# Per-tile waits for routed-row scatters, and a new order around them on VectorE and ScalarE

## The chip, the cores and the metric

The kernel runs on one core of a Trainium2 chip. The metric is the device time of one execution in microseconds (us). TensorE (PE) multiplies and transposes, VectorE (DVE) and ScalarE (ACT) work element by element, GpSimd (POOL) here mostly issues indirect DMAs, and SyncE (SP) issues the plain ones. Each engine runs its own list of instructions in order and waits on semaphores for the others. A change of 0.2% is 0.55 us.

## What is computed

An image batch of 4 x 128 x 16 x 16 passes a deformable-attention block, a self-attention block over 1024 tokens of 128 channels (8 heads of 16), and a layer of 16 experts with top-2 routing. The change lies between the last two, so only they are shown, cut to the core:

```python
t = t + attention(layernorm(t))                      # 4 images x 256 tokens x 128
x = layernorm(t).reshape(-1, 128)                    # "nrm": the rows that are routed
gate_logits = x @ gate_weight.T                      # 16 experts
top_vals, top_idx = top_k(gate_logits, 2)
routing_w = softmax(top_vals)
h = silu(einsum('td,efd->tef', x, w1))
h_mean = (sum of h over the tokens that chose expert e) / count_e
y_mean = einsum('ef,edf->ed', h_mean, w2)
t = t + sum_k routing_w[k] * y_mean[top_idx[k]]
```

## The kernel before

The 1024 tokens are 8 tiles of 128, in two halves: half 0 is tiles 0 to 3 (images 0 and 1), half 1 tiles 4 to 7. Self-attention runs in 8 units (image x group of four heads), pipelined by hand: step k of `unit_step` on each engine does the scores of unit k, the softmax of unit k - 1 and the outputs of unit k - 2, for k = 0 to 9 (UNITS is 8). Units 0 to 3 make half 0, units 4 to 7 half 1.

The outputs of a unit go this way: TensorE weighs the values (`weigh_values`), ACT copies the result out of PSUM (`unit_out`), TensorE turns it (`turn_out`, L1556), and DVE divides it by the sum of the softmax (`unit_norm`, L1063 the reciprocal and L1065 the multiply). When a half's four units are there, TensorE turns the half's outputs (`turn_outputs`, L1576), ACT copies them to `o_c` (`outputs_out`, L689), and TensorE makes from them the outputs' part of the gate logits (`output_logits`, L1588) and the projection (`project_out`, L1595).

From there a half goes to the experts. On DVE: `input_deviation` (L1081; for half 1 it waits for half 1's `output_logits`), `rank_logits` and `choose` (top 2 of each token), `residual` (L1072, the block's sum `x2_k`), `moments` (L807, L810). TensorE's `rank` (L1608 to L1612) counts, for each token, those before it that chose the same expert. DVE's `place` (L1111 to L1123) turns that into slot numbers, and `experts_of` (L1127 to L1133) notes which expert owns which slots. For the layer norm of the routed rows, ACT takes the root (`root`, L739), DVE the reciprocal and the shift (`scale`, L1139 and L1140), and ACT writes the four normalised tiles (`normalise`, L732), one increment of the semaphore `lnf["norm"]` for each tile.

POOL then scatters the rows: for each tile t and each of the two choices an indirect DMA (L509) writes 128 rows from `nrm` to their slots in DRAM (`scratch`), 16 scatters in all, tiles in order. When the eight scatters of a half have landed, SP reads that half's slots back in three groups of 512 rows (L418). TensorE turns them (`turn_slots`, L1680), ACT copies them (`columns_out`, L776), and each tile of 128 slots is multiplied with its experts' weights (`expert_tiles`, L1697 and L1705). Each tile holds four grains of 32 slots, each with an expert of its own; the weights of three of the four are first copied to fixed places ("staged"), six of these copies by ACT (`stage_first`, L759) and the rest by DVE (`stage`, L1199). ACT applies SiLU (L786); DVE's staging copies and TensorE's later tiles wait for earlier ones. The means, the second expert matrix, the sum over the routing weights and the stores end the kernel.

The order of the work around the change is written out by hand. On DVE it is: step 8 of `unit_step` (with `unit_norm(6)`, then half 0's `rank_logits`, `choose`, `residual`, `moments`), step 9 (only `unit_norm(7)`), `scale(0)`, `place(0)`, `experts_of(0)`, then half 1's `input_deviation` (L1081) and so on to `place(1, lambda: scale(1))`, which has the scale step inside it (`between`, after its second operation). On ACT: `root(0)`, `outputs_out(1)`, `normalise(0)`, two staging copies, `root(1)`, `normalise(1)`, the copies of x2, four staging copies, an exponential and a load of the SiLU table, then `columns_out(0)`. On TensorE: step 9 with `turn_out(7)`, `rank(0)` and `input_logits(1)`, then `turn_outputs(1)`, `output_logits(1)`, `project_out(1)`, `rank(1)`, `turn_x2`, and `turn_slots(0)`. POOL waits ahead of each half for its slot numbers (`slots_ready`) and for all four normalised tiles of the half.

## Time and profile before

| | us |
|---|---|
| median of 3 runs | 275.45 |
| the runs | 275.06 to 275.71 |
| the profiled execution, its own time | 275.87 |
| its span (first to last instruction) | 273.9 |

| engine | busy us | share of the span |
|---|---|---|
| PE, matmuls | 222.5 | 81% |
| PE, weight loads | 154.9 | 57% |
| DVE | 207.4 | 76% |
| ACT | 174.7 | 64% |
| POOL | 48.1 | 18% |

The time of the profiled execution is its span and some 2 us around it. The shares are averages over unlike stages. The stage of this change lies between 200 and 240 us, where no engine is full: there the waits between engines count, and the timelines of each engine show them. Times in the rows are us from the start of the span. TensorE's clock is given as a share of 2.4 GHz: 1.00 is 2.4 GHz and 0.50 is 1.2 GHz.

### The profile page before, as it was taken

How to read it: one execution, taken by the hardware profiler on the slowest of the kernel's cores; microseconds unless marked ns; L12 is line 12 of the kernel's file. 1: busy time of each engine (PE TensorE's matmuls, PEld its weight loads, DVE VectorE, ACT ScalarE, POOL GpSimd, SP SyncE). 2: the span in 40 equal slices, each digit the busy share in tenths (PEclk: the TensorE clock that was granted, in tenths of full speed). 3: DMA queues.
4: the chain of work that ended last, by engine and by line, in shares of the span. 5: the costliest groups of instructions: out<-in, count | busy, mean ns of one | idle time of the engine just before them, and what ended most of it. 6: DMA issues, size and time to landing. Idle time of an engine off the chain costs nothing.

```text
span 273.9 us, 7291 instructions
## 1 busy us (share of the span) xinstructions
PE 222.5 (81%) x2936; PEld 154.9 (57%) x2936; DVE 207.4 (76%) x482; ACT 174.7 (64%) x257; POOL 48.1 (18%) x64
## 2 busy tenths in 40 slices
PE   0799449999999998869999887889987307899985
PEld 0579327666767667637979755566556203233354
DVE  5766888999999999865335967888849957598412
ACT  5366898999999996066442567675667391565610
POOL 7004918910000000010001100000000677100000
PEclk9999859999999999997999999999999855999999
DMA  6930000000000000790000000000000115594002
GB/s 148 357 140 2 0 0 4 2 5 2 2 5 2 2 2 5 243 370 2 0 0 4 0 0 2 0 2 0 2 1 4 38 50 162 153 425 175 0 2 77
DMA packets 8590, 16.38 MB, mean 60 GB/s; under 512 B 752, under 2 KB 5104, under 8 KB 8304
## 3 DMA queue, kind: packets, MB, share of 16 engines
q1 hardware_dynamic: 8048, 14.90, 15.5%
q0 software_dynamic: 512, 1.05, 1.2%
q8 instruction: 23, 0.38, 0.6%
q14 instruction: 7, 0.06, 0.1%
HBM read 12.80 MB, written 3.15 MB: 58 GB/s over the span
## 4 chain that ended last, share of the span: by engine, by line
issue 54%; PE 30%; DVE 8%; ACT 3%; DMA 3%; SPq 1%; DVEq 1%; ACTq 0%
PE ps L1697 8%; PE ps L1380 6%; DVE wide L991 5%; PE ps L1720 2%; DVE msda L996 2%; DMA r_sb<-in_rows 2%; ACT arena L594 1%; PE ps L1760 1%; PE ps L1282 1%; PE ps L1680 1%; PE ps L1366 1%; PE ps L1335 1%; DMA late<-slot_rows 1%; PE ps L1311 1%; PE ps L1323 1%
## 5 line engine op out<-in xcount | busy, mean ns | idle before, releaser
L594 ACT ACTIVATE arena<-ps,one_less_sq 128x1024 bf16<-128x1024 f32 x64 | 67.2, 1112 | 4.7 <-PE ps L1366 4.7
L1380 PEld LDWEIGHTS ps<-arena 128*128 128x128 bf16 x1536 | 43.3, 96 | 19.8 <-issue 10.4
L1380 PE MATMUL ps<-arena 128*128 128x48 bf16 x1536 | 49.4, 184 | 5.1 <-DVE wide L991 4.6
L996 DVE TENSOR_REDUCE msda<-wide 128x768 f32 x32 | 46.1, 1513 | 0.0
L1366 PE MATMUL ps<-wide,sel 64*128 64x512 bf16 x128 | 25.7, 400 | 7.3 <-ACT arena L594 7.3
L991 DVE TENSOR_TENSOR wide<-ps,wide 128x768 f32<-128x768 f32 x32 | 30.1, 1009 | 1.1 <-PE ps L1380 1.1
L509 POOL DMA_INDIRECT slot_rows<-nrm,slots x16 | 16.1, 1006 | 66.2 <-ACT nrm L732 61.7
L1697 PE MATMUL ps<-arena,w_sb 128*32 x48 | 23.5, 636 | 1.0 <-ACT sel L786 1.0
L1046 DVE TENSOR_REDUCE t_k<-ps 128x2 f32<-128x512 f32 x32 | 20.5, 684 | 0.0
L668 ACT ACTIVATE wide<-ps 128x512 f32<-128x512 f32 x32 | 17.3, 594 | 1.4 <-PE ps L1526 1.3
L1705 PE MATMUL ps<-late,w_sb 128*32 128x512 f32 x80 | 16.6, 667 | 0.0
L1199 DVE COPY late<-arena 128x512 f32 x34 | 12.0, 423 | 4.8 <-PE ps L1705 3.0
L1021 DVE SCALAR_TENSOR_TENSOR wide<-ps,v_sb,wide 128x512 f32<-128x512 f32 x8 | 5.9, 750 | 11.8 <-ACT wide L640 9.2
L1039 DVE SCALAR_TENSOR_TENSOR xm<-ps,raw_by,xm 128x512 fp32r<-128x512 f32 x16 | 11.9, 748 | 3.7 <-ACT xm L657 1.9
L1697 PEld LDWEIGHTS ps<-arena,w_sb 128*32 128x32 f32 x48 | 5.4, 117 | 16.3 <-issue 16.3
L786 ACT ACTIVATE sel<-ps 128x512 f32<-128x512 f32 x12 | 6.9, 601 | 9.7 <-PE ps L1705 9.7
L1680 PE MATMUL ps<-ident,late 128*128 128x128 f32 x24 | 4.5, 330 | 10.1 <-DMA late<-slot_rows 10.1
L1366 PEld LDWEIGHTS ps<-wide,sel 64*128 64x128 bf16 x128 | 6.2, 93 | 11.1 <-ACT arena L594 7.7
L660 ACT ACTIVATE xm<-ps,high_by 128x512 fp32r<-128x512 f32 x8 | 5.5, 686 | 10.5 <-PE ps L1488 10.5
L495 POOL MEMSET t_k<- 128x1024 f32 x1 | 1.0, 952 | 63.4 <-PE ps L1426 63.4
L640 ACT ACTIVATE wide<-ps,v_sb 128x512 f32<-128x512 f32 x8 | 5.4, 694 | 9.6 <-PE ps L1444 9.6
L1680 PEld LDWEIGHTS ps<-ident,late 128*128 128x128 f32 x24 | 3.2, 166 | 13.0 <-issue 13.0
(320 smaller groups left out, 510.7 us busy)
## 6 DMA issues: line engine op xcount, KB each, us to landing
arena<-in_w_t SPq DMA_DIRECT2D x1, 4096.0 KB, 13.6
wide<-in_w_t SPq DMA_DIRECT2D x1, 4096.0 KB, 15.2
w_sb<-in_weights SPq DMA_DIRECT2D x1, 1544.0 KB, 8.8
slot_rows<-t_c SPq DMA_DIRECT2D x2, 768.0 KB, 10.4
late<-slot_rows SPq DMA_DIRECT2D x6, 256.0 KB, 3.3
x_sb<-in_x SPq DMA_DIRECT2D x4, 128.0 KB, 2.3
out<-xn SPq DMA_DIRECT2D x4, 128.0 KB, 1.8
r_sb<-in_rows SPq DMA_DIRECT2D x1, 288.0 KB, 4.7
```

Of the source, the lines that this page charges most:

```text
L509: nc.gpsimd.indirect_dma_start(out=scratch[h], out_offset=bass.IndirectOffsetOnAxis(ap=slots[:, c, t:t + 1], axis=0), in_=nrm[:, t, :], in ...
L594: nc.scalar.activation(hot[:, u, c:c + 5:4, :, :], ps[:, 2 * (c % 2):2 * (c % 2) + 2, :].rearrange("r p (b q) -> r p b q", b=B), ACT.Relu, ...
L668: nc.scalar.activation(prob_t[u % 2][:, i, :], ps[:, 2 + i % 2, :], ACT.Exp).then_inc(prob_ready, 1)
L991: nc.vector.tensor_tensor(prod[:, c, :, :, :], g, w.unsqueeze(3).to_broadcast([P, 2, NP * NK, DH]), ALU.mult).then_inc(g_free, 1)
L996: nc.vector.tensor_reduce(msda[:, 4 * c + u:4 * c + u + 3:2, bass.ds(i, 1), :].rearrange("q b h d -> q b (h d)"), prod[:, c, :, :, :].rear ...
L1039: nc.vector.scalar_tensor_tensor(out=to, in0=ps[:, 6 + of_keys, :].rearrange("c (n t) -> c n t", n=2), scalar=raw_by[:, of_keys:of_keys + ...
L1046: nc.vector.tensor_reduce(nmax[:, :, 2 * (u % 2) + i // 2, HROWS * (i % 2) + SPLIT], ps[:, i % 2, :].rearrange("q (t k) -> q t k", t=2), A ...
L1199: nc.vector.tensor_copy(staged_at[n % len(staged_at)], w1_sb[:, bass.ds(at[q][t % GROUP], 1), :].rearrange("d e f -> d (e f)")).then_inc(s ...
L1366: ins = nc.tensor.matmul(ps[:, 2 * (c % 2) + a, :], sel[rows, i % 4, c, :], terms_t[rows, i // 4, u * HALF:(u + 1) * HALF])
L1380: ins = nc.tensor.matmul(ps[:, 4 + b, p * NK * DH:(p + 1) * NK * DH], hot[:, u, p, b, :], rhs, start=(s == 0), stop=(s == PARTS - 1))
L1697: nc.tensor.matmul(ps[0:GRAIN, 2 + t % 4, :], x_cols[:, t * P:t * P + GRAIN], w1_sb[:, bass.ds(at[j], 1), :].rearrange("d e f -> d (e f)"))
L1705: ins = nc.tensor.matmul(ps[GRAIN * q:GRAIN * (q + 1), 2 + t % 4, :], x_cols[:, t * P + GRAIN * q:t * P + GRAIN * (q + 1)], staged_at[entr ...
```

## The change

- POOL waits for the normalised rows of one tile ahead of that tile's two scatters, and for the slot numbers once in a half, as before.
- On ACT `normalise(0)` comes ahead of `outputs_out(1)`.
- On DVE step 9 of `unit_step` does nothing any more; `place(0)` comes directly after step 8, with `scale(0)` inside it as half 1 has it, and `unit_norm(7)` follows it, ahead of `experts_of(0)`.

```diff
@@ POOL
                 h = t // 4
                 if t % 4 == 0:
                     pool.wait_ge(slots_ready, h + 1)
-                    pool.wait_ge(lnf["norm"], 4 * (h + 1))
+                pool.wait_ge(lnf["norm"], t + 1)
@@ ACT
             root(0)
+            normalise(0)
             outputs_out(1)
-            normalise(0)
@@ DVE, unit_step
-                if k >= 2:
+                if 2 <= k <= UNITS:
                     unit_norm(k - 2)
@@ DVE
-            scale(0)
-            place(0)
+            place(0, lambda: scale(0))
+            unit_norm(UNITS - 1)
             experts_of(0)
```

## Rows read from the trace of the kernel before

**Rows 1.** Chain that ended last, in order of time: start us, us, what.

```profile
224.85 2.78 DMA late<-slot_rows
...
236.02 0.61 ACT sel L786
```

**Rows 2.** Timeline of POOL, 180 to 232: start us, us, instruction [idle before <-releaser].

```profile
213.32 1.22 POOL L509 DMA_INDIRECT slot_rows<-nrm,slots  x1 [61.66 <-ACT nrm L732]
...
222.41 1.08 POOL L509 DMA_INDIRECT slot_rows<-nrm,slots  x1 [0.31 <-issue]
223.79 0.96 POOL L509 DMA_INDIRECT slot_rows<-nrm,slots  x1 [0.30 <-issue]
```

**Rows 3.** Timeline of ACT, 180 to 246.

```profile
209.14 0.30 ACT L739 ACTIVATE lnf_std<-lnf_mv,eps_c 128x4 f32<-128x4 f32 x1 [0.89 <-DVE lnf_mv L810]
210.30 0.60 ACT L689 ACTIVATE xn<-ps 128x512 f32<-128x512 f32 x1 [0.87 <-PE ps L1576]
210.80 1.64 ACT L732 ACTIVATE nrm<-t_k,lnf_shift,lnf_rstd 128x128 f32<-128x128 f32 x4
...
218.32 1.65 ACT L732 ACTIVATE nrm<-t_k,lnf_shift,lnf_rstd 128x128 f32<-128x128 f32 x4 [0.63 <-issue]
...
228.97 0.60 ACT L776 ACTIVATE w_sb<-ps 128x512 f32<-128x512 f32 x1 [2.93 <-PE ps L1680]
```

**Rows 4.** Instructions of the tile nrm, 205 to 235: ns min/median/max, first and last start.

```profile
L732 ACT ACTIVATE nrm<-t_k,lnf_shift,lnf_rstd x8: 478/482/493, 210.8 to 219.5; 128x128 f32<-128x128 f32 x8
```

**Rows 5.** Timeline of DVE, 180 to 246.

```profile
209.02 0.17 DVE L1063 RECIPROCAL inv_sum<-ps 128x8 f32<-128x8 f32 x1
...
209.76 0.17 DVE L1111 TENSOR_SCALAR quads_e<-ps 128x16 f32<-128x16 f32 x1
...
210.42 0.42 DVE L1117 TENSOR_REDUCE first_slot<-quads_before 128x16 f32<-128x256 f32 x1
...
211.46 0.29 DVE L1123 TENSOR_REDUCE slots<-picked_slot 128x8 int32<-128x128 f32 x1
...
213.01 0.22 DVE L1081 TENSOR_TENSOR lg<-ps,ln_std 128x64 f32<-128x64 f32 x1
...
217.91 0.18 DVE L1139 RECIPROCAL lnf_rstd<-lnf_std 128x4 f32<-128x4 f32 x1
218.12 0.16 DVE L1140 SCALAR_TENSOR_TENSOR lnf_shift<-lnf_mv,lnf_rstd 128x4 f32<-128x4 f32 x1
218.20 0.41 DVE L1117 TENSOR_REDUCE first_slot<-quads_before 128x16 f32<-128x256 f32 x1
...
219.23 0.29 DVE L1123 TENSOR_REDUCE slots<-picked_slot 128x8 int32<-128x128 f32 x1
...
232.40 0.76 DVE L1199 COPY msda<-arena 128x512 f32 x2
```

**Rows 6.** Timeline of PE, 180 to 246.

```profile
208.63 0.25 PE L1612 MATMUL ps<-pair_sq,ones_b 128*128 128x64 bf16 x4
...
209.63 0.64 PE L1576 MATMUL ps<-ident,msda 128*128 128x128 f32 x4
210.95 1.06 PE L1588 MATMUL ps<-gate_o,xn 128*128 128x16 f32 x8 [0.69 <-ACT xn L689]
211.87 1.14 PE L1595 MATMUL ps<-w_sb,xn 128*128 128x128 f32 x8
215.50 0.18 PE L1608 MATMUL ps<-ceil_b,ones_b 128*128 128x16 bf16 x1 [2.49 <-DVE pair_sq L1104]
...
227.84 1.94 PE L1680 MATMUL ps<-ident,late 128*128 128x128 f32 x8 [10.09 <-DMA late<-slot_rows]
...
236.86 0.61 PE L1697 MATMUL ps<-arena,w_sb 128*32 x1 [1.05 <-ACT sel L786]
```

**Rows 7.** Stretches: busy us of PE, PEld, DVE, ACT, POOL, granted clock, DMA share, GB/s.

```profile
212.00:218.00 6.00, 2.98 (x23) 2.29 (x22) 5.55 (x33) 1.88 (x5) 3.77 (x4) 0.87 0.11 33
...
232.00:234.00 2.00, 2.00 (x16) 0.52 (x12) 1.16 (x4) 0.00 (x0) 1.68 (x2) 0.62 0.11 33
```

## The prediction

> **What bounds the kernel now.** I read the chain of work that ended last first. From the reload of the routed rows on it is one piece: a 256 KB read-back (2.78 us) issued at 224.85, TensorE's transposes of those rows at 227.84, expert tiles 0 to 3, the first SiLU at 236.02, expert tile 4 at 236.86, and from there TensorE nearly without a hole [rows 1, 6]. TensorE stood idle for 10.09 us ahead of 227.84 and was released by that read-back [rows 6], so everything after it moves with the read-back. The read-back waits for the eight scatters of half 0, so the timeline of POOL comes next: the first scatter starts at 213.32, the eighth ends at 222.41 + 1.08 = 223.49, and the ninth (half 1) follows with a gap of 0.30 [rows 2]. POOL's own work is a closed queue of one scatter per (223.79 - 213.32) / 8 = 1.31 us, and the read-back lands 4.14 us after the eighth ends (224.85 + 2.78 = 227.63). What sets the end is therefore when the first scatter starts.
>
> Its releaser is read in the timelines of ACT and DVE. The four normalisations of half 0 start at 210.80 and end at 212.44 [rows 3], each 0.48 long [rows 4]; the slot numbers of half 0 start at 211.46 and are there at 211.75 [rows 5]. POOL starts 213.32 - 212.44 = 0.88 after the last of them. The row of tile 0 was ready at 210.80 + 0.48 = 211.28.
>
> **The change part by part, in the profiled execution.**
>
> *Wait of one tile.* The first scatter needs the slot numbers (211.75) and tile 0's row (211.28), no longer the fourth row (212.44). Alone: 212.44 - 211.75 = 0.69 earlier. The rows follow at under 0.41 us each, the scatters at two per tile, so no later tile waits. Six more waits are executed, three in half 0. The trace doesn't show POOL executing a met wait apart from its instruction; the gap of 0.30 between scatters is the nearest row, so three of them cost 0 to 0.9 us at the most; I take 0, since the ninth scatter, at which the kernel before passes both of its waits, has the same 0.30 ahead of it as the eighth [rows 2]. The start-up of 0.88 stays; a wake-up by DVE may differ from one by ACT, for which I allow one such gap, 0.3, either way.
>
> *DVE.* The last unit's reciprocal and multiply leave the place ahead of half 0's slot numbers. They and the scale step take 209.76 - 209.02 = 0.74, the scale step 0.29 of it, so the two are 0.45. The chain of place took from 209.76 to 211.75, that is 1.99; with the scale step inside it takes 1.99 + 0.29 (217.91 to 218.20, where half 1 already runs so) = 2.28 [rows 5]. It now begins at 209.02, so the slot numbers are there at 211.30, 0.45 earlier. The scale step comes 0.66 into the chain (209.76 to 210.42), at 209.68; the root that it needs ended at 209.44 [rows 3], so it doesn't wait, and rank(0) ended at 208.63 + 0.25 = 208.88 [rows 6]. The shift is ready after 0.21 and 0.16 more (217.91, 218.12), at 210.05.
>
> *ACT.* Normalisation follows the shift by 0.04 (218.12 + 0.16 = 218.28, then 218.32, in half 1 [rows 3, 5]) and starts at 210.09 instead of 210.80; tile 0's row is there at 210.57, the fourth at 211.73. All rows now precede the slot numbers or their own scatter. This part gives nothing by itself; it is needed, because the outputs' copy now waits for a late transpose and would hold the rows to 213.1.
>
> Sum on the path: first scatter 0.88 after 211.30, at 212.18: **1.14 us earlier** than 213.32. The read-back and TensorE's restart follow at 226.70.
>
> *What is paid: half 1.* The unit's multiply ended at 209.52, 0.50 after its reciprocal began; that now begins 0.20 after the last operation of place starts (211.01), so the multiply ends at 211.71. TensorE's transposes of half 1's outputs start at 211.83 instead of 209.63, the copy on ACT at 212.50 instead of 210.30, the outputs' logits at 213.15 instead of 210.95, each step with its old distance [rows 3, 6]. DVE is done with experts_of(0) at 213.01 as before (the same instructions in another order) and then waits for these logits (about 1.06 long, so 214.27): the next step slips from 213.01 by D = 1.26 [rows 5, 6]. Queued behind it on DVE are half 1's choice, residual, moments, slot numbers, the gap, and the staging copies; on TensorE rank(1) and turn_x2; on ACT root, normalise(1), x2_out, four staging copies and two table loads. All slip by D.
>
> Who waits for that? (a) POOL's ninth scatter, wanted at 222.65: half 1's slot numbers end at 219.52 + D = 220.8, and tile 4's row earlier still, so 1.9 us are left. (b) ACT must be free for the copy of the first transposed rows. It started that copy at 228.97 after 2.93 of idle [rows 3], free since 226.04: slack 2.93 before, 2.93 - 1.14 = 1.79 with TensorE 1.14 earlier. (c) DVE's staging copies for tile 4, done by 232.40 + 0.76 = 233.16, against 236.86 [rows 5, 6]: slack 3.7, later 2.6. So the gain on the path is min(1.14, 2.93 - D), and with D = 1.26 all of 1.14 arrives.
>
> *The clock.* The new idle stretches of TensorE run from about 209.7 (the transposes that began at 209.63 now come later) to 211.83 and 212.5 to 213.15, with the later one (213.01 to 215.50 before [rows 6]) shrinking to about 1.4. In the trace the granted clock averages 0.87 over 212 to 218, so it fell from 2.4 to 1.2 GHz at about 216.4, after that long idle stretch; it rose at about 233.5 (mean 0.62 over 232 to 234), with TensorE at work from 227.84 [rows 6, 7]. With a long idle stretch now 213.01 - 209.7 = 3.3 us earlier, the fall may come that much earlier, around 213, on the outputs' logits of half 1. At 1.2 GHz eight passes of this kind take 1.94 (the transposes at 227.84) instead of 1.06 [rows 6], so D goes up to 1.26 + 0.9 = 2.2, and the gain is 2.93 - 2.2 = 0.75. The fall can land anywhere between, so I take the middle of 1.14 and 0.75: **0.95 us**. The Trainium skill (TensorE: Matmul & The Clock Gate, HAM oscillation) says that idle between bursts sends the array back to the low clock; it speaks against this change, which puts a hole in work that was dense, and the rows of the fall at 216.4 agree.
>
> *A second rule against it.* The scatters that ran beside DVE's staging copies took 0.96 to 1.08 (those at 223.79 and 222.41 [rows 2]); the first, beside small operations, took 1.22. The copies are now D later and the scatters 1.14 sooner, so fewer scatters of half 0 stand beside a copy; I take nothing, bound +0.12, the 1.08 over the 0.96. The Trainium skill (DMA: Bandwidth & Descriptors, SWDGE vs HWDGE vs iDMA) says that DVE in its two-port mode locks GpSimd out of the SBUF in which it writes its descriptors; by that the scatters beside the copies would grow, and the rows show no more than the 0.12.
>
> **The rivals.**
> 1. *The clock takes or gives the difference.* TensorE restarts 1.14 earlier, but its first four tiles run at 1.2 GHz until the rise. If the rise stays at 233.5, the time from 226.70 to 233.5 is 6.8 at half rate instead of 5.7: only 0.57 arrives, 274.9. If it comes 2 us sooner than the restart's shift explains, another 1.0 is saved: 2.1 in all, 273.3. For: the trace shows one such rise, and nothing ties it to the restart. Together 0.25, about equal parts.
> 2. *Slower: the half-1 work on ACT becomes the bound.* Place: the copy of the first transposed rows behind ACT's table loads, which end at 226.04 + D. It decides from D = 2.93. If the low clock holds over the outputs' logits, their projection, rank and the transposes of x2, and each of these is waited for in turn, D is 1.26 + 0.9 + 1.0 + 0.8 = 4.0 and the kernel is 1.1 slower, 276.5. Against: projection (old start 211.87) runs beside DVE's choice, which hides it. 0.11.
> 3. *The edit doesn't move the first scatter.* If POOL's 0.88 isn't a wake-up but work that ended independently of ACT, or if the extra waits cost the 0.9, then 0 to 0.3 is left: 275.3. For: nothing in the trace tells what the 0.88 is. 0.10.
> 4. *The first SiLU isn't released by TensorE's start.* Tile 0's products come first of four tiles after 227.84, yet the SiLU that reads them starts at 236.02 [rows 1], when TensorE is through with all four. If what holds them is not bound to the restart, nothing arrives: 275.4. For: I can't explain the hold; against: it ends just as TensorE's burst ends, which moves. 0.06.
>
> **How the numbers follow.** The profiled execution took 275.87 (span 273.9 and 1.97 around it), 0.42 above the median 275.45; the shift is taken off the median: 275.45 - 0.95 = 274.5. Chance of this case 0.48, with its own range 274.0 to 274.9. Range for 8 in 10: down to the early rise (273.3, less 0.1 for a D of 1.26) and up to the rival without effect, 275.7. A change of 0.2% is 0.55 us, about what a measurement can tell from none: faster means under 274.9, slower over 276.0. Faster: 0.48 less 0.05 at its edge, 0.13 and 0.06 of rival 1, 0.62 in all; slower: rival 2 and scatter of runs, 0.12; the rest 0.26.
>
> **What would show it.** First scatter near 212.2, started by DVE's slot numbers and not by ACT; eight scatters of 1.31; read-back near 223.7; transposes near 226.7; the first SiLU about 1 us earlier. DVE idle about 1.2 (full clock) to 2.2 us ahead of L1081, released by TensorE's L1588. ACT's copy of the first transposed rows with under 2 us idle before it; none left means D reached 1.79. The prediction is wrong if the first scatter stays at 213.3, if that copy waits for ACT, or if the clock's rise moves by more than the restart.

## The result and the profile after

The changed kernel takes 279.87 us (median of 5 runs, 279.44 to 281.49) against 275.45 for the kernel before: the ratio is 1.0161, with a 95% interval of 1.0113 to 1.0208. It is 4.4 us slower, where 0.95 us faster was predicted. The profiled execution of after took 279.87 with a span of 277.8, 3.9 us more than the span of before. The ratios and intervals here and below leave out executions over 1.5% above the fastest of their kernel; the lists of runs show all.

The page of after, its span and busy times:

```profile
span 277.8 us, 7292 instructions
...
PE 228.5 (82%) x2936; PEld 158.4 (57%) x2936; DVE 207.4 (75%) x482; ACT 175.3 (63%) x257; POOL 47.9 (17%) x64
```

VectorE and ScalarE do the same work as before. TensorE shows 6 us more for the same 2936 instructions: more of them ran at the low clock. That is no cause yet: it can follow from new waits just as well.

I read after in the order of the prediction's sum. The timeline of POOL (start us, us, instruction, [idle before <-releaser]), first and ninth scatter:

```profile
212.26 1.22 POOL L509 DMA_INDIRECT slot_rows<-nrm,slots  x1 [60.45 <-ACT nrm L732]
...
222.72 0.96 POOL L509 DMA_INDIRECT slot_rows<-nrm,slots  x1 [0.30 <-issue]
```

The first scatter starts 1.06 earlier than in [rows 2]; 1.14 was predicted (212.18). The queue is as closed as before: (222.72 - 212.26) / 8 = 1.31. So what the change is about arrived. TensorE's timeline, from half 1's outputs to the next tiles:

```profile
211.90 0.66 PE L1576 MATMUL ps<-ident,msda 128*128 128x128 f32 x4 [1.98 <-DVE msda L1065]
213.25 1.80 PE L1588 MATMUL ps<-gate_o,xn 128*128 128x16 f32 x8 [0.69 <-ACT xn L689]
...
226.59 2.17 PE L1680 MATMUL ps<-ident,late 128*128 128x128 f32 x8 [6.14 <-issue]
231.54 1.05 PE L1697 MATMUL ps<-arena,w_sb 128*32 x1 [2.77 <-issue]
...
237.92 0.66 PE L1680 MATMUL ps<-ident,late 128*128 128x128 f32 x4
...
239.65 1.05 PE L1705 MATMUL ps<-t_k,w_sb 128*32 128x512 f32 x3
...
244.32 0.66 PE L1680 MATMUL ps<-ident,late 128*128 128x128 f32 x4
```

Half 1's transposes start at 211.90 (211.83 predicted). The restart is at 226.59 (226.70 predicted, 227.84 in [rows 6]), 1.25 ahead of before. But then the expert tiles, which followed the transposes directly in before, start at 231.54: 2.77 us of idle have come between them. Tile 4 begins at 239.65 where before had it at 236.86, and the next group's transposes stand at 244.32 against 240.43. From there to the end the distance stays 3.9. **All of the loss arises between 228.8 and 244.3**, and the reason is in what ACT and DVE did there. The places in before that I compare with, on TensorE and DVE:

```profile
229.72 1.06 PE L1697 MATMUL ps<-arena,w_sb 128*32 x1
```

```profile
225.88 0.16 DVE L1180 TENSOR_SCALAR expert_of<-expert_of 128x12 f32<-128x12 f32 x1
...
231.72 0.76 DVE L1199 COPY t_k<-arena 128x512 f32 x2 [1.46 <-issue]
```

ACT in after:

```profile
228.23 0.20 ACT L772 ACTIVATE table_junk<-eps_c 128x1 f32<-128x1 f32 x1
230.80 0.60 ACT L776 ACTIVATE w_sb<-ps 128x512 f32<-128x512 f32 x1 [2.37 <-remote]
235.10 0.60 ACT L776 ACTIVATE w_sb<-ps 128x512 f32<-128x512 f32 x1 [3.71 <-remote]
235.59 1.08 ACT L786 ACTIVATE sel<-ps 128x512 f32<-128x512 f32 x2
```

ACT is free at 228.43. The transposes that its two copies wait for ended by 226.59 + 2.17 = 228.76, the first four of them about half way. Yet the copies start at 230.80 and 235.10. In before the first of them started as soon as four transposes were through (228.97, [rows 3]). DVE:

```profile
228.27 0.16 DVE L1180 TENSOR_SCALAR expert_of<-expert_of 128x12 f32<-128x12 f32 x1
229.38 0.56 DVE L1181 TENSOR_TENSOR t_k<-expert_of,expert_f 128x384 f32<-128x384 f32 x1 [0.95 <-DVE expert_of L1180]
...
232.20 0.17 DVE L1129 TENSOR_TENSOR end_slot<-end_slot,first_slot 128x16 f32<-128x16 f32 x1 [2.07 <-remote]
233.61 0.36 DVE L1130 TENSOR_TENSOR ended<-end_slot,slot_no 128x192 f32<-128x192 f32 x1 [1.24 <-DVE end_slot L1129]
235.01 0.35 DVE L1132 TENSOR_REDUCE expert_of<-ended 128x12 f32<-128x192 f32 x1 [1.04 <-DVE ended L1130]
...
239.17 0.76 DVE L1199 COPY t_k<-arena 128x512 f32 x2 [1.47 <-issue]
```

This is `experts_of(1)` and the counts after it, a chain in which each instruction waits for an increment of DVE's own semaphore by the one before. At L1181 the releaser is DVE's own L1180, which was done at 228.43, and the wait lasts until 229.38. Four such waits add up to 0.95 + 2.07 + 1.24 + 1.04 = 5.3 us. In before the same instructions follow each other without a wait. So an instruction waits for an increment whose producer is through, 1 to 2 us on DVE (from itself) and longer on ACT (from TensorE): the first copy starts some 3 us after its four transposes were through, the second 6.3 us after the last transpose. I call this **the hold** below. POOL is in the second half of its scatters then. The view of waits, 226 to 241 (engine, line <- releaser: us in total, times, longest), shows the same from the other side:

```profile
ACT w_sb L776 <- remote: 6.1, 2, 3.7
...
DVE end_slot L1129 <- remote: 2.1, 1, 2.1
...
PEld ps L1705 <- DVE t_k L1199: 1.2, 2, 1.0
```

"Remote" means that no instruction of this core's engines ended just ahead of the release. No other core runs here, so I read the word as the mark of a late arrival, not of a sender.

### The profile page after: what moved, and what is told of

It reads as the page before. It is cut to its first block, busy times and chain, and to the rows that moved or that the text cites. A ratio compares the mean times of both kernels' runs of the same rounds, so it can differ in the third digit from the quotient of the medians.

```text
span 277.8 us, 7292 instructions
## 1 busy us (share of the span) xinstructions
PE 228.5 (82%) x2936; PEld 158.4 (57%) x2936; DVE 207.4 (75%) x482; ACT 175.3 (63%) x257; POOL 47.9 (17%) x64
## 4 chain that ended last, share of the span: by engine, by line
PE 48%; DVE 20%; issue 17%; ACT 9%; DMA 2%; DVEq 1%; SPq 1%; ACTq 1%; another core or an unknown queue 1%
PE ps L1380 5%; PE ps L1697 5%; DVE wide L991 4%; DVE t_k L1046 3%; PE ps L1488 3%; PE ps L1454 3%; PE ps L1541 2%; PE ps L1720 2%; DVE msda L996 2%; PE ps L1502 2%; PE ps L1266 2%; PE ps L1705 2%; PE ps L1514 2%; PE ps L1444 2%; DMA r_sb<-in_rows 2%
## 5 line engine op out<-in xcount | busy, mean ns | idle before, releaser
L996 DVE TENSOR_REDUCE msda<-wide 128x768 f32 x32 | 45.1, 1452 | 0.0
L991 DVE TENSOR_TENSOR wide<-ps,wide 128x768 f32<-128x768 f32 x32 | 29.1, 948 | 1.2 <-PE ps L1380 1.2
L1697 PE MATMUL ps<-arena,w_sb 128*32 x48 | 24.9, 659 | 2.8 <-issue 2.8
L1705 PE MATMUL ps<-late,w_sb 128*32 128x512 f32 x80 | 18.0, 688 | 0.0
L1488 PE MATMUL ps<-z_h,wqk_h 128*128 128x256 f32 x32 | 10.4, 325 | 0.0
```

Source lines behind the costliest of these rows:

```text
L991: nc.vector.tensor_tensor(prod[:, c, :, :, :], g, w.unsqueeze(3).to_broadcast([P, 2, NP * NK, DH]), ALU.mult).then_inc(g_free, 1)
L996: nc.vector.tensor_reduce(msda[:, 4 * c + u:4 * c + u + 3:2, bass.ds(i, 1), :].rearrange("q b h d -> q b (h d)"), prod[:, c, :, :, :].rear ...
L1488: ins = nc.tensor.matmul(ps[:, 6 + of_keys, j * HW:(j + 1) * HW], w[:, at_w:at_w + P], z[:, b * HW:(b + 1) * HW], start=(n == 0), stop=(n ...
L1697: nc.tensor.matmul(ps[0:GRAIN, 2 + t % 4, :], x_cols[:, t * P:t * P + GRAIN], w1_sb[:, bass.ds(at[j], 1), :].rearrange("d e f -> d (e f)"))
L1705: ins = nc.tensor.matmul(ps[GRAIN * q:GRAIN * (q + 1), 2 + t % 4, :], x_cols[:, t * P + GRAIN * q:t * P + GRAIN * (q + 1)], staged_at[entr ...
```

## The experiments

Executions of one kernel vary here by up to 7 us; those of the kernel before lie between 274.95 and 279.56, 19 of all 79 at 278.6 and above. That upper group reaches the times of after, and none of its executions was profiled, so whether it is the same loss isn't known. The work ahead of the first scatter varies by over 1 us from one profile to the next with nothing changed in it. So traces are compared from a common point, the first scatter: its start, and the tail from there to the end of the span. The "first SiLU" column is its distance from the first scatter. Ratios are against the kernel before, run beside each on the same chip. Each row of the trace columns is one execution, and not always a typical one.

| kernel | first scatter | first SiLU | tail | span | ratio of the times [95%] |
|---|---|---|---|---|---|
| before | 213.32 | +22.70 | 60.6 | 273.9 | 1 |
| after | 212.26 | +23.33 | 65.5 | 277.8 | 1.0161 [1.0113, 1.0208] |
| e1_waits_alone | 212.35 | +22.82 | 60.6 | 273.0 | 0.9988 [0.9935, 1.0042] |
| e2_orders_alone | 213.91 | +22.98 | 60.9 | 274.8 | 1.0125 [1.0031, 1.022] |
| e3_pe_kept_busy | 213.64 | +23.21 | 64.8 | 278.4 | 1.0136 [1.0045, 1.0226] |
| e4_half1_scatters_late | 213.79 | +19.11 | 66.6 | 280.4 | 1.0241 [1.0141, 1.0342] |
| e5_few_increments_after | 211.22 | +23.20 | 66.1 | 277.3 | 1.0118 [1.0032, 1.0204] |
| e6_few_increments_before | 214.56 | +22.85 | 60.7 | 275.3 | 1.0019 [0.9964, 1.0074] |
| e7_waits_few_increments | 212.99 | +22.75 | 62.3 | 275.3 | 0.9979 [0.9934, 1.0024] |
| e8_half1_late_by_filler | 211.80 | +22.80 | 65.1 | 276.9 | 1.0109 [1.006, 1.0158] |
| e9_clock_kept_before | 215.00 | +26.87 | 67.6 | 282.6 | 1.0223 [1.0135, 1.031] |
| e10_twelve_scatters | 213.73 | +19.91 | 62.4 | 276.1 | 0.9992 [0.9944, 1.0041] |
| e11_chain_ahead_after | 212.54 | +23.35 | 64.2 | 276.7 | 1.0217 [1.0125, 1.0309] |
| e12_chain_ahead_waits | 214.34 | +23.02 | 60.9 | 275.2 | 1.001 [0.998, 1.004] |
| e13_twelve_scatters_before | 214.66 | +18.15 | 58.2 | 272.9 | 0.9949 [0.9924, 0.9974] |
| e14_clock_kept_shorter | 214.59 | +24.25 | 66.1 | 280.7 | 1.0165 [1.0045, 1.0285] |
| e15_dve_chain_late | 214.52 | +22.95 | 62.5 | 277.0 | 0.9997 [0.9946, 1.0047] |

**The parts alone: e1 and e2.** e1 is the kernel before with the new waits on POOL alone, e2 the changed kernel with the old waits, that is the new orders on DVE and ACT alone.

```diff
                     pool.wait_ge(slots_ready, h + 1)
-                    pool.wait_ge(lnf["norm"], 4 * (h + 1))
+                pool.wait_ge(lnf["norm"], t + 1)
```

> The kernel before with the wait for one tile's rows as its only change. The trace of the changed kernel shows its first scatter 1.06 us earlier, as forecast, and yet 4 us lost, most of it behind increments of semaphores by TensorE and VectorE that other engines see 1 to 2 us late between 228 and 235 us. Theory A (held increments are set off by where the scatters of half 1 stand against TensorE's turning of the slots and VectorE's chain of small operations): the scatters are only 0.7 us earlier and VectorE's chain isn't late, so the result is open between -0.7 us (no longer hold than before) and +2 (hold moves onto VectorE's chain as well). Theory B (the loss comes from half 1's work being 2.15 us late): -0.7 us, 274.8. First scatter at 212.6.

> The changed kernel with the old wait for all four rows: only the new orders on VectorE and ScalarE. The first scatter starts at 212.7 (0.88 after the fourth row at 211.86). Theory B (half 1's lateness makes the loss): within 0.5 us of the changed kernel, 279.4 to 280.3, with L1081 at 215.2. Theory A (the place of the scatters against the chains decides): anything between 275 and 280, with a hold that shows as idle time of VectorE in its linked operations or of ScalarE ahead of L776.

In e1's trace the first scatter starts 0.97 earlier than in before and the span is 0.9 shorter, with the tail the same. ACT's first SiLU in e1:

```profile
235.17 2.07 ACT L786 ACTIVATE sel<-ps 128x512 f32<-128x512 f32 x4 [5.42 <-PE ps L1705]
```

It has the idle time of [rows 1] again ahead of it and has moved by 0.85. So the path argument holds for the waits, though ten runs (274.49 to 278.31) don't separate the gain of the times from nothing. e2 took 276.88 to 281.46 and is slower by its times, but its profiled execution was its fastest run, with a tail of only 60.9: DVE's chain lost 0.5 in it and ACT nothing. Half 1 was as late in it as in after (L1081 2.96 after the first scatter, 2.90 in after) and the staging copies for tile 4 started 22.27 after the first scatter, 3.87 later than in before, at no cost. So in this execution the lateness stayed within the slack that the prediction reckoned. The loss comes with the new orders, then, and not in every execution. How much of the 1.0161 the waits add to e2's 1.0125 these intervals don't tell.

**The clock: e3.** The changed kernel with dummy multiplications on TensorE in its idle stretches, so that it keeps 2.4 GHz over half 1's logits.

```diff
+            keep_clock(9, 2)
             turn_outputs(1)
+            keep_clock(3, 2)
             output_logits(1)
             project_out(1)
+            keep_clock(5, 2)
             rank(1)
```

> The changed kernel with dummy bf16 multiplications of TensorE into an unused PSUM bank in its new idle stretches: 9 ahead of the turn of half 1's outputs, 3 ahead of the outputs' logits, 5 ahead of rank(1). The granted clock should stay at 2.4 GHz over half 1's logits, so L1081 slips by 1.26 instead of 2.15 us. Theory B: half 1's lateness makes the loss, so 1 us or more comes back, under 279.0. Theory A: what is held isn't bound to this lateness, so the gain is anything from 0 to 4 by where the hold falls; if the hold stays and shows the same idle times (2.4 and 3.7 us ahead of L776), under 0.9 us comes back.

The clock stayed at 2.4 GHz until about 222, and L1081 came 215.80 - 213.64 = 2.16 after the first scatter instead of 2.90 in after. The tail is 64.8, the ratio 1.0136. ACT's copies (L776) still stood for 2.72 and 3.00 and DVE's chain for some 4.4. The fall of the clock ahead of half 1's logits is not what costs the 4.4 us, unless the dummies cost what the clock gives back, which this run can't exclude.

**The scatters: e4.** The changed kernel with POOL's ninth scatter held back until ACT has made both of its copies.

```diff
                     pool.wait_ge(slots_ready, h + 1)
+                if t == 4:
+                    pool.wait_ge(cols_ready, 2)
```

> The changed kernel, but the eight scatters of half 1 start only when ScalarE has copied the first two groups of slots. No scatter runs beside TensorE's first turning of slots and VectorE's second experts_of. Theory A (scatters in flight hold the increments of TensorE and VectorE): the idle of ScalarE ahead of its two copies L776 falls from 2.4 and 3.7 us to under 1.5 and 0.5, and VectorE's linked operations L1181, L1129, L1130, L1132 lose their waits of 1 to 2 us. Theory C (the hold is independent of the scatters, of the read-back or of a queue of semaphores): the waits stay. The whole time is longer in both, because the read-back of half 1 comes late; only the holds are looked at.

ACT's copies and the first SiLU, then a step of DVE's chain, then the ninth scatter (lines are 2 higher than in after):

```profile
230.19 1.06 ACT L778 ACTIVATE w_sb<-ps 128x512 f32<-128x512 f32 x2
...
232.90 0.60 ACT L788 ACTIVATE sel<-ps 128x512 f32<-128x512 f32 x1 [1.65 <-PE ps L1707]
```

```profile
231.10 0.18 DVE L1131 TENSOR_TENSOR end_slot<-end_slot,first_slot 128x16 f32<-128x16 f32 x1
```

```profile
232.37 0.95 POOL L511 DMA_INDIRECT slot_rows<-nrm,slots  x1 [8.52 <-issue]
```

With no scatter running, both of ACT's copies go back to back, DVE's chain has no wait, and the first SiLU stands 19.11 after the first scatter instead of 22.70, in the kernel before, or 23.33. As soon as the scatters resume, waits of this kind come back: the fourth SiLU, at 240.90, has 3.99 of idle ahead of it. Half 1 is late now, so the kernel as a whole is slower (282.47 and 282.92). **The hold goes with the scatters.**

**The number of increments: e5, e6, e7.** TensorE's transposes of slots and of x2 increment a semaphore eight and four at a time; here only the last of each four does. e5 is the changed kernel so, e6 the kernel before, e7 the kernel before with the new waits.

```diff
-            nc.tensor.transpose(slots_bank(g)..., x_slots[...], ident[:, :]).then_inc(cols_mm, 1)
+            ins = nc.tensor.transpose(slots_bank(g)..., x_slots[...], ident[:, :])
+        ins.then_inc(cols_mm, 1)
...
-        act.wait_ge(cols_mm, GROUP * g + GROUP)
+        act.wait_ge(cols_mm, g + 1)
```

> The changed kernel with one increment for each group of four transposes (turn_slots and turn_x2) instead of four. Without half 1's scatters in flight the holds were gone, so the scatters cause them. Theory A1 (TensorE's increments queue up behind the scatters and are let out one at a time, some 1.4 us apart, and VectorE's linked operations wait in the same queue): with a quarter of the increments the copy of the first group starts within 0.6 us of ScalarE being free, the second within 1.5 us of its transposes, VectorE's chain loses less than 2 us instead of 5, and the kernel takes 275 to 277.5. Theory A2 (the hold belongs to the stretch of the scatters alone, however many increments there are): the idle times and 279 to 281 stay.

> The kernel before with one increment for each four transposes. The runs of the kernel before lie in two groups, 275.0 to 276.2 and 278.6 to 279.4. A1: the upper group becomes rare and the median of the lower one stays within 0.4 us of 275.4. A2: both groups stay with about a third of the runs in the upper.

> The kernel before with the wait for one tile's rows and with one increment for each four transposes. A1: 274.4 to 275.2, below both kernels, with few runs over 276. A2: as the wait alone, whose ten runs lie between 274.5 and 278.3 with a median of 276.65.

Nothing of substance moved. e5 is as slow as after (279.25 to 281.28), with 2.64 and 2.97 ahead of ACT's copies and 1.21, 1.72 and 2.08 in DVE's chain. e6 equals the kernel before, and in e7, too, the first SiLU keeps its +22.75. The Trainium skill (VectorE: DVE Perf Modes, the section on the TRN2 errata) warns that a high rate of increments by one engine can deadlock another, and that dense increments by several engines should be spaced. Nothing deadlocked here; if the hold were a mild form of that, e5 and e6 should have lost it, and they didn't. e7's profile shows one thing more, in the view of stretches (busy us of PE, PEld, DVE, ACT, POOL, clock, DMA share, GB/s):

```profile
238.00:240.00 2.00, 2.00 (x16) 0.54 (x12) 1.93 (x6) 1.38 (x3) 0.00 (x0) 0.50 1.23 391
```

TensorE, idle for 2.17 ahead of tile 4, fell back to 1.2 GHz for about 3.4 us, where it stood at 1.00 in the kernel before. At half rate that is some 1.7 us (an estimate from these rows), as much as e7's tail of 62.3 is over 60.6.

**Lateness alone: e8.** The kernel before with DVE's order and POOL's waits untouched, the new order on ACT, and dummy multiplications ahead of half 1's transposes, so that half 1 comes late with TensorE's clock up.

```diff
             root(0)
-            outputs_out(1)
             normalise(0)
+            outputs_out(1)
...
+            keep_clock(10, 2)
             turn_outputs(1)
```

> The kernel before with ScalarE's new order, and with ten dummy multiplications of TensorE ahead of the turn of half 1's outputs; VectorE's order and the wait for four rows stay. Half 1's logits come about 2.1 us late as in the changed kernel, with TensorE at 2.4 GHz, and the first scatter starts at about 212.7. Theory L (the loss is made by half 1's lateness, which puts TensorE's increments and VectorE's second chain into the stretch in which the scatters hold them): 278 to 281, as the new orders alone (276.9 to 281.5). Rival (it is the new order on VectorE or the low clock that loses): within 1 us of the kernel before, under 276.5.

The logits ran at the high clock, and DVE's chain was held:

```profile
212.28 1.06 PE L1588 MATMUL ps<-gate_o,xn 128*128 128x16 f32 x8 [0.69 <-ACT xn L689]
```

```profile
231.75 0.56 DVE L1181 TENSOR_TENSOR t_k<-expert_of,expert_f 128x384 f32<-128x384 f32 x1 [1.85 <-remote]
...
234.54 0.17 DVE L1234 TENSOR_TENSOR cnt<-cnt,cnt_half 128x16 f32<-128x16 f32 x1 [1.98 <-remote]
...
237.17 0.76 DVE L1199 COPY t_k<-arena 128x512 f32 x2 [1.46 <-issue]
```

```profile
237.65 1.59 PE L1706 MATMUL ps<-t_k,w_sb 128*32 128x512 f32 x3 [1.16 <-DVE t_k L1199]
```

The tail is 65.1, the ten runs lie between 278.57 and 281.7, and the ratio is 1.0109 [1.006, 1.0158]. Neither the new waits nor DVE's new order is in this kernel, and its dummies end at 211.2, ahead of the first scatter. **Half 1 being late is enough** for two thirds of the loss by the times, though not in every execution (e2's profile). The path is DVE's chain: it lost 4.9 in four held waits, the staging copies for tile 4 came 25.37 after the first scatter, and TensorE waited for them until +25.85, 2.3 later than in before. ACT's own copies were held for under 1 us, and the first SiLU kept its +22.80. The tail is 4.5 longer than that of before, but up to 1.7 of this is another fall of the clock (0.50 over 238 to 240), which after doesn't have.

**The clock raised for the tiles: e9 and e14.** The kernel before with ten dummy multiplications between `project_out(1)` and `rank(1)`, and more of them (40 in e9, 14 in e14) ahead of `turn_slots(0)`, to raise the clock for tiles 0 to 3.

```diff
             project_out(1)
+            keep_clock(10, 2)
             rank(1)
...
+            keep_clock(40, 2)
             turn_slots(0)
```

> The kernel before with dummy multiplications of TensorE ahead of rank(1) (10) and ahead of the first turning of slots (40), so that it restarts at 2.4 GHz or gets there sooner. Theory H: the first SiLU is released by the end of the hold, 22.7 us after the first scatter, and not by TensorE's speed, so nothing is gained: 275.0 to 276.5, with a longer wait of ScalarE ahead of the first SiLU. Rival C (the low clock over the first four tiles is on the path): 1.4 to 2.8 us faster, 272.6 to 274.1.

TensorE turned to the slots only at 237.97, so e9 says nothing on the clock. But it shows the hold in a new place. Of the 40 dummies 35 were through by 228.62, 0.22 each, and at that pace the last five would have ended at 229.7, about when the read-back was there. Instead each of the five stood, and DVE's chain with them:

```profile
233.68 0.59 PE L1388 MATMUL ps<-ones_b,ident_b 128*128 128x512 bf16 x1 [1.75 <-issue]
235.85 0.58 PE L1388 MATMUL ps<-ones_b,ident_b 128*128 128x512 bf16 x1 [1.58 <-issue]
237.27 0.58 PE L1388 MATMUL ps<-ones_b,ident_b 128*128 128x512 bf16 x1 [0.83 <-issue]
```

```profile
235.14 0.18 DVE L1234 TENSOR_TENSOR cnt<-cnt,cnt_half 128x16 f32<-128x16 f32 x1 [2.75 <-remote]
235.87 0.17 DVE L1235 TENSOR_SCALAR cnt<-cnt 128x16 f32<-128x16 f32 x1 [0.55 <-DVE cnt L1234]
237.26 0.25 DVE L1236 RECIPROCAL inv_cnt<-cnt 128x16 f32<-128x16 f32 x1 [1.22 <-DVE cnt L1235]
```

The kernel gives these dummies no semaphore to wait for and none to increment. So the hold isn't only on increments that come late: it also stops instructions of TensorE that wait for nothing in the kernel, and both engines go on at the same instants (235.85 and 235.87, 237.27 and 237.26). And since TensorE sends no increment in this stretch, its increments aren't the cause of DVE's waits.

> The kernel before with dummy multiplications of TensorE ahead of rank(1) (10) and ahead of the first turning of slots (14 instead of 40). TensorE restarts with the read-back as in the kernel before. Theory H: its clock doesn't matter, the first SiLU comes at 22.7 after the first scatter and the span ends at 60.6 to 60.9. Rival C (the clock over the first four tiles is on the path): 1 us or more sooner. If turn_x2 is late through the first ten, x2_out on ScalarE still has 2 us of slack.

e14 took 282.77, 282.18, 284.18 and 278.44. Its profiled execution is one of the long ones:

```profile
232.58 0.17 DVE L1235 TENSOR_SCALAR cnt<-cnt 128x16 f32<-128x16 f32 x1 [0.53 <-issue]
233.29 0.25 DVE L1236 RECIPROCAL inv_cnt<-cnt 128x16 f32<-128x16 f32 x1 [0.53 <-DVE cnt L1235]
234.01 0.20 DVE L1237 TENSOR_SCALAR in_quad<-quad_i 128x64 f32<-128x64 int32 x1 [0.47 <-issue]
```

```profile
236.10 0.60 ACT L776 ACTIVATE w_sb<-ps 128x512 f32<-128x512 f32 x1 [8.79 <-remote]
```

ACT stood idle for 8.79 ahead of this copy. Some 2.8 of it is the ordinary wait for the four transposes, which began at 228.98; the other 6.0 are hold, about as long as the longest one otherwise (6.19 in e11). DVE's chain was held for 1.65 + 0.53 + 0.53 + 0.47 + 1.19 = 4.4, although DVE and ACT have the order of before. I had expected at worst no change. The dummies ended at 221.47, well ahead of the hold, and the fourth run took 278.44, so one trace doesn't show that they cause it. The clock stood at 0.50 over 228 to 242 all the same, so neither e9 nor e14 tests rival C, a faster clock over the first tiles; that stays untested.

**Fewer scatters: e10 and e13.** Tiles 6 and 7 aren't scattered, so 12 scatters run instead of 16; e10 is the changed kernel so, e13 the kernel before.

```diff
-                for c in range(TOPK):
+                for c in range(TOPK if t < 6 else 0):
...
-            sp.wait_ge(scattered[h], 16 * 4 * TOPK)
+            sp.wait_ge(scattered[h], 16 * (4, 2)[h] * TOPK)
```

> The changed kernel without the four scatters of tiles 6 and 7, so their rows are missing in the sums of the experts. In all traces so far held increments of TensorE come through 22.7 us after the first scatter starts, about 2.2 us after the sixteenth ends. Theory H (the hold lasts as long as the stream of scatters and begins in its last quarter): with twelve scatters the stream ends 15.4 us after its start, nothing is held at 16 to 22.7 us; ScalarE copies the first group of slots as soon as it is free, VectorE's linked operations have no waits over 0.3 us, the first SiLU comes within 3 us of TensorE's first expert tile, and the kernel takes under 276, up to 4 us less than the changed kernel. Rival (the scatters are not the cause, it is the read-back or the queue of increments itself): the waits stay and so do 279 to 281.

> The kernel before without the four scatters of tiles 6 and 7 (their rows are missing in the experts' sums). I read each run from its first scatter on, because what lies ahead of it varies by 1.4 us from run to run: in the kernel before and three variants the span ends 60.6 to 60.9 us after the first scatter starts, with the first SiLU at 22.7. Theory H: the hold goes, the first SiLU starts right after tile 0's products, at 18.5 to 19.5, and tile 4 starts as soon as TensorE is through with tile 3 and the next transposes, so the span ends 1 to 2 us sooner, 58.6 to 59.6 after the first scatter. Rival (the hold is hidden in the kernel before): 60.6 to 60.9.

e10, ACT's copies of the first two groups:

```profile
230.91 1.08 ACT L776 ACTIVATE w_sb<-ps 128x512 f32<-128x512 f32 x2
```

They don't wait, and no wait above 0.56 is left in DVE's chain; the first SiLU stands at +19.91. Against the kernel before with its 16 scatters the ratio is 0.9992 [0.9944, 1.0041], where it was 1.0161; the median, 276.87, still misses the "under 276" that I expected. And in e13, the kernel before without the four scatters:

```profile
230.36 0.60 ACT L776 ACTIVATE w_sb<-ps 128x512 f32<-128x512 f32 x1 [2.97 <-PE ps L1680]
...
232.81 0.60 ACT L786 ACTIVATE sel<-ps 128x512 f32<-128x512 f32 x1 [1.00 <-PE ps L1705]
```

The first SiLU comes when TensorE has made its first product, at +18.15 and no longer at +22.70. So the kernel before is held as well: this is what 4.6 of the 5.6 us ahead of its first SiLU were. By the tails the hold costs it 60.6 - 58.2 = 2.4 us, by the times 0.5% [0.3, 0.8], 1.4 us.

e13 is also the kernel that e10 has to be compared with, and there the loss isn't all gone: e10's runs have a median of 276.87 (275.61 to 278.55), e13's of 274.82 (273.37 to 275.34). That is 2.1 us by the medians, 1.2 by the two ratios, and 4.2 by the tails of two single executions (62.4 and 58.2; e10's is one of its long ones). Of the 4.4 us some 2.3 to 3.2 go with the four scatters; 1.2 to 2.1 stay. The traces show where. In e10 ACT gets to its copies only at 230.91, straight from its table loads, 17.18 after the first scatter instead of e13's 15.70, and DVE's staging copies for tile 4 are later still:

```profile
237.47 0.76 DVE L1199 COPY t_k<-arena 128x512 f32 x2 [1.47 <-issue]
```

That is +23.74, against +18.30 in e13, and TensorE takes tile 4 up at +24.25 instead of +21.17. I read this so: with 16 scatters the held first SiLU hides a part of half 1's lateness, and once it comes at +18 to +20, the lateness is more than the slack. A little hold is left in e10 too and adds to it: ACT's second copy of x2 starts 0.57 late at 225.19, given as "remote", and DVE's first staging copies come at +13.31, where they stand at +11.83 in after.

**The chain moved ahead: e11 and e12.** `experts_of(1)` and the counts stand ahead of the staging copies for tiles 1 to 3 instead of behind them, in the changed kernel (e11) and in the kernel before with the new waits (e12).

```diff
+            slot_experts(0)
+            experts_of(1)
+            slot_experts(1)
...
             dve.wait_ge(ld_w1, 16)
             dve.wait_ge(x2_mm, TILES)
...
-            slot_experts(0)
-            experts_of(1)
-            slot_experts(1)
```

> The changed kernel with VectorE's second chain (slot_experts, experts_of(1), the counts, 4.2 us of it) moved ahead of its first staging copies, so it runs 10 to 14 us after the first scatter instead of 16 to 25 us. Theory H: VectorE's chain loses nothing any more (5.3 us of waits in the changed kernel), its copies for tile 4 are ready by the time TensorE wants them, and what is left of the loss is ScalarE's copy of the slots behind TensorE's held increments: 276.5 to 279. Rival (VectorE's chain was covered by the hold of TensorE anyway): 279 to 281 as before the move.

> The kernel before with the wait for one tile's rows and the same move of VectorE's second chain. If the upper group of runs (278.6 to 279.4 in the kernel before, 276.4 to 278.3 with the wait alone) comes from VectorE's chain reaching into the hold, it goes: 274.3 to 275.3, below both kernels. If it comes from TensorE's increments or from the clock, both groups stay as with the wait alone, median 276.65.

A miss: I had looked for the hold from some 15 us behind the first scatter on. In e11 the chain runs from +10 on and is held from +13 to +19, for 1.35, 0.47, 0.46, 1.18 and 1.20; ACT's second copy is held for 6.19, up to 235.39; the staging copies come at 238.05. Its runs lie between 278.74 and 283.96. In e12 the new order neither costs nor brings anything that can be told apart (1.001 [0.998, 1.004]).

**DVE's chain late alone: e15.** The kernel before with six copies without use (2.2 us) ahead of the chain, so that it stands where the changed kernel has it, while ACT and TensorE are as before.

```diff
+            for n in range(6):
+                spare = (y_rest, hat_x, pair)[n % 3]
+                ins = nc.vector.tensor_copy(spare[:, :, :], y_pos[:, :, :])
+                if n % 3 == 2:
+                    link(ins)
             slot_experts(0)
             experts_of(1)
```

> The kernel before with six extra copies (2.2 us) on VectorE ahead of slot_experts(0) alone: VectorE's second chain runs as late as in the changed kernel (15 to 19 us after the first scatter), while TensorE's half 1, ScalarE and the scatters keep their times. Theory V (the loss of the changed kernel is VectorE's chain of linked operations standing in the hold): waits of 1 to 2 us show inside the chain, the copies for tile 4 are late, and the span ends 63 to 66 us after the first scatter; runs 278 to 281. Theory T (TensorE's own late work brings it): the chain is 2.2 us late, hidden by the slack of 3.7 us, and the span ends at 60.6 to 60.9; runs as before.

```profile
233.87 0.25 DVE L1241 RECIPROCAL inv_cnt<-cnt 128x16 f32<-128x16 f32 x1 [0.92 <-DVE cnt L1240]
```

The chain reaches into the hold only with its end and loses 0.92 + 0.93. The staging copies for tile 4 start 22.45 after the first scatter, 4.05 later than in before, and that is hidden behind ACT's held SiLU (ratio 0.9997 [0.9946, 1.0047]). The profile has a tail of 62.5. Up to 1.7 of it (the same estimate) is a fall to 1.2 GHz as in e7:

```profile
239.00:242.00 3.00, 3.00 (x16) 0.81 (x13) 3.00 (x10) 2.00 (x5) 0.00 (x0) 0.50 1.23 309
```

So DVE late by 2.2 is not enough when the hold takes only 1.85 from it. In e8 DVE's chain started as late (L1180 at +14.78, +14.77 here, +12.56 in before) but lost 4.9, and that was enough with ACT's copies hardly held. With 16 scatters what decides seems to be whether the copies for tile 4 come before or after the moment TensorE wants them, some 23.5 after the first scatter: +22.27 in e2 and +22.45 here, +25.37 in e8.

## Why the prediction was wrong

**What was right.** The part of the wait and of DVE's order: first scatter 212.26 for 212.18, eight scatters of 1.31, TensorE's restart 226.59 for 226.70. Half 0's slot numbers were there at 211.12 + 0.29 = 211.41 for 211.30, the whole chain of that execution being some 0.15 later. What was left open on the clock came out at its dear end, and correctly priced:

```profile
212.00:214.00 2.00, 1.31 (x8) 1.08 (x9) 1.31 (x5) 0.60 (x1) 1.44 (x2) 0.84 0.00 0
214.00:218.00 4.00, 3.06 (x16) 2.77 (x17) 2.64 (x18) 1.15 (x2) 3.09 (x4) 0.50 0.21 66
```

The granted clock fell at about 213.4, about 3 us earlier than in before, and the logits took 1.80 instead of 1.06. The delay of half 1 on DVE was this:

```profile
215.16 0.23 DVE L1081 TENSOR_TENSOR lg<-ps,ln_std 128x64 f32<-128x64 f32 x1 [1.71 <-PE ps L1588]
```

D = 215.16 - 213.01 = 2.15, with 2.2 forecast for the low clock. The price of slack (b), ACT's table loads, held too: ACT was free at 228.43, for 226.04 + 2.2 = 228.24 by the sum, and 0.54 ahead of where its first copy stood in before. Without a hold about that much of the gain could have passed ACT, where 0.75 was forecast for the low clock.

**The step that failed** is the sentence that everything after TensorE's restart moves with it, and with it the term min(1.14, 2.93 - D) for the gain. It rests on each increment reaching its waiter at once. From 228.4 on that wasn't so, and I had the sign in front of me: the kernel before had 5.60 us ahead of its first SiLU [rows 1] for a product that TensorE had made by 230.57 + 1.06 = 231.63, 4.4 us earlier. I gave that rival, 4, a chance of 0.06, and let its price be "nothing arrives". The place was right and the price wrong. e4, e10 and e13 show that the wait is bound to the scatters. In before, e1, e2, e6, e7, e8, e12 and e15 it ends 22.7 to 23.0 us after the first of them, 1.5 to 2.4 us after the sixteenth. TensorE's restart keeps its distance from the first scatter in these traces too (14.4 to 14.6), so they alone don't tell the two apart; e13 does, where the restart stands at +14.57 and the SiLU comes at +18.15. So the end of the wait moves with the scatters, and an earlier first scatter should arrive by it, as 0.85 of it did in e1's trace.

**Slack (c)** failed with it, and this is the term that turned a lost gain into a loss. DVE's staging copies for tile 4 were given 3.7 us of slack against a start of 236.86. The slack was read in a trace in which the chain ahead of these copies ends at 230.26, 16.9 after the first scatter, about where DVE's instructions begin to be held in after (its wait at L1181 runs from +16.2 to +17.1). In after half 1's work on DVE is 2.15 late, 2.4 by L1180 (228.27 for 225.88), and the scatters are 1.06 early. The chain starts 16.0 after the first scatter instead of 12.6 and runs into the hold:

| from the first staging copy for tile 4 | us |
|---|---|
| before, 231.72 | |
| half 1 late, D as it stands at L1180 | +2.4 |
| four held increments, 5.3, less the small gaps and durations that stood there before | +5.1 |
| after, 239.17 | +7.45 |

The slack of 3.7 is used up twice. On TensorE's side the sum runs to the same point: its tiles started 231.54 - 229.72 = 1.82 later (ACT's copy held for 2.37), and took 0.87 longer to the end of tile 3 and the four transposes behind it (231.54 to 238.51 against 229.72 to 235.82), since the clock rose only at about 237.3, later in the burst. So TensorE was ready for tile 4 at 238.51 and waited for DVE's copy until 239.65. From there DVE is the bound:

```profile
240.52 2.77 DVE L1199 COPY late<-arena 128x512 f32 x8
```

A copy is 0.34 in a row of them, so three per tile are 1.01, while TensorE took 0.86 per tile there in before (237.31 to 238.17). With no copies made ahead any more, the stretch from tile 4 to the next group's transposes took 244.32 - 239.65 = 4.67 instead of 240.43 - 236.87 = 3.56, another +1.1. Together 2.8 + 1.1 = 3.9, the difference of the spans.

In terms of the common point: first scatter -1.06, first SiLU relative to it +0.63 (held by ACT's second copy until 235.10), and from the first SiLU to the end 42.2 instead of 37.9, +4.3; in sum +3.9.

**Two held paths end close together** at tile 4: DVE's copies at 239.65, TensorE with ACT's held copies at 238.51. This is worked out from one trace. Without DVE's waits at most 239.65 - 238.51 and the 1.1 behind it would be won back, 2.2 of 3.9; e11, which has the chain moved ahead and ACT's copy held for longer, won 1.3 of its tail and nothing by its times. DVE's lateness can be hidden (e15) or be the whole path (e8), by how much of it the hold adds. And taking most of the hold from both wins back 2.3 to 3.2 us of the times, not all (e10 beside e13): the rest is half 1's lateness with what little hold e10 has left, and the prediction had put that lateness at nothing as long as each slack was larger than D.

**The rivals.** Rival 1, the clock: the rise neither stayed nor came sooner, it came 3.8 later than in before, in a burst that itself started later. The prediction named a rise that moves by more than the restart as a sign of being wrong, and it was one. Rival 2, ACT behind its table loads, asked for D = 2.93; D was 2.15, and ACT stood idle there for another reason. (In e10, where the hold is mostly gone, ACT does go from its table loads straight into the copy.) Rival 3 didn't occur. The range (273.2 to 275.7) had no case in it that cost more than 0.3 us, and the dearest rival outside it cost 1.1, because each slack was reckoned against a single engine's start and none of them against the scatters, the one thing that ran beside them all.

**What stays open.** That the hold needs the scatters in flight is shown (e4, e10, e13); by what mechanism they do it isn't. Its end is steady. Its beginning isn't: in before ACT took an increment of TensorE at +15.6, in after one sent at about +15.4 had not come at +16.2, when ACT was free for it, in e11 and e9 the hold began at +13 to +14, and in e10 one wait of 0.57 ended at +11.5. How much of the loss half 1's lateness alone would cost with 16 scatters and no hold wasn't measured either. Nor did I find why executions of one kernel fall into groups 2 to 4 us apart, in the kernel before too, or why e2's profiled execution escaped. A version that keeps e1's earlier scatter and is measurably faster than before wasn't found: e1, e7 and e12 all have intervals that hold 1.

## What to carry to other kernels

A wait that lasts for microseconds after its producer was done is a cost with a cause of its own: before working out a sum, ask which traffic runs beside it, and measure once without that traffic, as e13 does, with both kernels and not only one. A slack read in a trace holds only for the time window in which it was read; a change that puts one engine's wait ahead of the other half's work shifts that work, here by 2.15 us, against everything that keeps its place or moves the other way. Where executions vary by more than the effect, compare them from a common event, such as the first scatter.

## What the hardware showed that I had not expected

- While indirect scatters follow each other at 1.31 us, and for about 2 us after, instructions of TensorE, VectorE and ScalarE are held. Even an instruction that waits for the one directly ahead of it on the same engine, for 0.03 to 0.05 in before, waited for 1.0 to 2.1 in after, and in e9 dummy multiplications that wait for nothing in the kernel stood for 0.83 to 1.75.
- The held instructions go on in step, whatever their engine. In e14 they went on at 231.88, 232.58, 233.29, 234.01, 235.40 (DVE), 236.10 (ACT) and 236.84 (TensorE): one, or once two, steps of 0.70 to 0.74. In after they went on at 229.38 (DVE), 230.80 (ACT), 231.54 (TensorE), 232.20, 233.61 and 235.01 (DVE), which are about one or two such steps. The scatters' own pace, 1.26 to 1.31, is not a multiple of it. I take this for the trace of one thing that serves the engines in turn, but no run tells what it is.
- This doesn't show in any busy time. The Trainium skill (Perfetto Trace Analysis, "The 4-stage abstract model" and the timelines behind it) says that the profile shows an instruction's execution and not the propagation of its semaphore update. The trace agrees: producers end on time, and only the idle time ahead of the held instructions, up to 6.19 us in e11, tells of it.
- Dummy multiplications on TensorE, put in to keep its clock, came with longer times (e9: 281.95 to 284.59; e14: 282.2 to 284.2 in three of four runs, 278.44 in the fourth). In e9 they were held themselves; in e14 the cause isn't shown.
- TensorE's clock fell to 1.2 GHz at about 213.4, with idle stretches of 1.98 and 0.69 ahead of it in the trace, where in before it fell only behind one of 2.49. In e7, e8 and e15 it fell again for about 3.4 us near 238 to 242, behind idle stretches of 2.17, 1.16 and 2.64; at half rate that costs up to 1.7 us each, by estimate. In e12 and e2, with 1.38 and 1.97 in that place, it stood at 1.00.
